# Output products of an attention kernel one unit later, with their operands a unit ahead and the weights' operands spread between the adds

## The reference

```
x  = hidden states, 4 batches x 512 tokens x 1024, f32
xn = layernorm(x)
qkv = xn @ w_qkv             32 query heads, 8 key and 8 value heads, 128 wide
scores = q k^T / sqrt(128) - slope(head) * sqrt(distance), causal
attn = softmax(scores) @ v
out = x + attn @ w_o + (xn @ W^T + b + the chosen low-rank term of xn)
```

## Time and profile before

| | |
|---|---|
| three runs | 2558.04, 2558.14 (median), 2559.82 us |
| the profiled execution | 2558.13 us, its span 2556.3 us |
| PE busy | 2429.0 us, 95% |
| DVE busy | 1593.5 us, 62% |
| ACT busy | 1442.5 us, 56% |
| POOL busy | 884.0 us, 35% |
| granted PE clock, mean | 0.987 |

### The profile page before, as it was taken

One profiled execution on the slowest core, in us unless ns is written; L12 is line 12 of the kernel. 1 busy time (PEld: TensorE's weight loads), 2 busy tenths in 40 slices (PEclk: granted clock), 3 DMA queues, 4 the chain that ended last, 5 costly groups with the idle time before them and its releaser, 6 DMA issues.

```text
span 2556.3 us, 35119 instructions
## 1 busy us (share of the span) xinstructions
PE 2429.0 (95%) x12128; PEld 2042.3 (80%) x12128; DVE 1593.5 (62%) x2905; ACT 1442.5 (56%) x3131; POOL 884.0 (35%) x1158
## 2 busy tenths in 40 slices
PE   6999999997999999998899999999999999999998
PEld 4787888885778888887788888888888888888886
DVE  6657445565756445654666777667766776667765
ACT  4432133334533133333877777777777777777774
POOL 3211000001231000000464556545654556445654
PEclk8999999998999999999999999999999999999999
DMA  4546354464355435445613231332334231332221
GB/s 148 183 132 222 116 191 159 176 219 176 103 159 202 153 137 198 169 176 189 227 67 116 102 121 68 115 116 100 110 146 182 100 116 67 124 115 101 80 108 69
DMA packets 94704, 355.25 MB, mean 139 GB/s; under 512 B 8874, under 2 KB 9018, under 8 KB 85569
## 3 DMA queue, kind: packets, MB, share of 16 engines
q1 hardware_dynamic: 62480, 233.43, 25.5%
q0 software_dynamic: 32048, 119.60, 13.5%
HBM read 235.02 MB, written 117.97 MB: 138 GB/s over the span
## 4 chain that ended last, share of the span: by engine, by line
PE 79%; DVE 10%; issue 5%; ACT 4%; DMA 1%; POOL 1%; ACTq 0%; DVEq 0%; SPq 0%; POOLq 0%
PE ps L648 25%; PE ps L650 25%; PE ps L649 25%; PE ps L835 4%; DVE wo L1130 3%; DVE acc L1398 1%; ACT probs L1049 1%; DVE probs L1367 1%; DVE pt_lo L1130 1%; ACT wo L895 1%; ACT res_hi L895 1%; DVE stats L1144 1%; ACT rows L924 1%; DVE w_lo L1130 1%; DMA qk_s<-res_hi 0%
## 5 line engine op out<-in xcount | busy, mean ns | idle before, releaser
L895 ACT ACTIVATE w_hi<-raw 128x1024 fp32r<-128x1024 f32 x196 | 207.0, 1059 | 559.3 <-PE ps L650 440.8
L1130 DVE TENSOR_TENSOR w_lo<-raw,w_hi 128x1024 fp32r<-128x1024 f32 x196 | 239.1, 1224 | 358.2 <-ACT w_hi L895 358.1
L1398 DVE TENSOR_TENSOR acc<-ps,acc 128x512 f32<-128x512 f32 x448 | 296.7, 684 | 226.7 <-issue 195.4
L648 PE MATMUL ps<-x_hi,w_hi 128*128 128x512 f32 x1120 | 436.3, 390 | 0.0
L650 PE MATMUL ps<-x_hi,w_lo 128*128 128x512 f32 x1120 | 435.8, 389 | 0.0
L649 PE MATMUL ps<-x_lo,w_hi 128*128 128x512 f32 x1120 | 435.7, 389 | 0.0
L648 PE MATMUL ps<-wo,op_hi 128*128 128x512 f32 x896 | 367.0, 410 | 50.4 <-issue 30.6
L1035 ACT ACTIVATE probs<-probs,neg_max 128x512 f32<-128x512 f32 (+3 forms) x512 | 283.6, 565 | 200.8 <-DVE neg_max L1367 200.8
L650 PE MATMUL ps<-wo,op_lo 128*128 128x512 f32 x896 | 354.8, 396 | 0.0
L649 PE MATMUL ps<-wo,op_hi 128*128 128x512 f32 x896 | 353.1, 394 | 0.0
L1367 DVE CUSTOM_DVE_ANT_0 probs<-ps,bias 128x512 f32<-128x512 f32 (+3 forms) x512 | 220.3, 484 | 95.3 <-PE ps L650 93.3
(11 more groups left out here) (156 smaller groups left out, 4983.9 us busy)
## 6 DMA issues: line engine op xcount, KB each, us to landing
raw<-w_all SPq DMA_DIRECT2D x70, 1024.0 KB, 5.5
q<-qk_s SPq DMA_DIRECT2D x128, 512.0 KB, 3.3
qk_s<-res_hi POOLq DMA_DIRECT2D x40, 1024.0 KB, 4.6
wo_raw<-w_o SPq DMA_DIRECT2D x64, 512.0 KB, 5.5
qk_s<-res_a POOLq DMA_DIRECT2D x20, 1024.0 KB, 9.1
qk_s<-res_b POOLq DMA_DIRECT2D x20, 1024.0 KB, 5.3
k<-qk_s SPq DMA_DIRECT2D x32, 512.0 KB, 5.7
v<-v_s SPq DMA_DIRECT2D x32, 512.0 KB, 8.5
```

The lines of the kernel that those rows point to most:

```text
L648: pe.matmul(to, st_hi, mv_hi, start=start, stop=False, skip_group_check=True)
L895: nc.scalar.activation(to, source, ACT.Copy).then_inc(signal, 1)
L1130: nc.vector.tensor_tensor(to, source, high.bitcast(F32), ALU.subtract).then_inc(signal, 1)
L1398: nc.vector.tensor_tensor(to, fill[f % 2][:, :], to, ALU.add).then_inc(s_acc, 1)
```

## The change

The order of the units stays (pair of batches, key head, batch, head; `unit` is written in another way), and so do the number and shape of all instructions. What moves:

- `fills`: each part is one unit later. The four parts of a set that were at places 1 and 5 are now at places 2 and 6, and so on; the loop has one more turn at its end.
- `shaped`: all `op_hi` and `op_lo` and the differences of a part are made in the unit ahead of it; nothing is made in its own unit.
- the weights: highs of steps 0, 1 at the end of place 4 (before: 3); 3, 2 at the end of 5; 4, 5 at the start of 6, ahead of the first exponential; 6 at the end of 6. Lows of 0, 1 and 3 at the end of place 5 (there are three parts there); step 2 at place 6 behind `pt_lo`; 4 between the adds of place 6; 5 and 6 behind its last add. Sums: 4 at place 3, 2 and 3 at place 4, 5 at place 5. Before: lows 0, 1 at the end of 3; 2, 3, 4 at the end of 4; 5, 6 at the end of 5.
- SP's issue of the next group's blocks keeps its place in the program (place 7), and its condition.
- the running sums go out and come in a tile pair at a time, in turns of SP of their own.

```
-OUT_SPLITS = ((), (0, 1), (2, 3, 4), (5, 6))
-WO_SUMS_IN = ((4,), (2,), (3, 5), ())
+WO_SUMS_IN = {7: (4,), 8: (2, 3), 9: (5,)}
+WO_ORDER = (0, 1, 3, 2, 4, 5, 6)
+HIGHS_FIRST = {10: (4, 5)}
+HIGHS_LAST = {8: (0, 1), 9: (3, 2), 10: (6,)}
+LOWS_EARLY = {10: (2,)}
+LOWS_MIDDLE = {9: (0, 1), 10: (4,)}
+LOWS_LAST = {9: (3,), 10: (5, 6)}
...
         def fills(n):
-            s, c = (n - 1) // G - 1, (n - 1) % G
+            s, c = (n - 2) // G - 1, (n - 2) % G
...
         def shaped(n):
-            s, c = n // G - 1, n % G
...
+            s, c = (n - 1) // G - 1, (n - 1) % G
...
+            return s, [OUT_SUMS[i] for i in SUM_SHARES[c]], list(SHARES[c])
...
+        def making(n, table):
+            group, place_ = (n - 3) // GROUP_UNITS, (n - 3) % GROUP_UNITS + 7
+            return [(group, i) for i in table.get(place_, ())] if 0 <= group < GROUPS else []
...
-                if n % (2 * G) == G + 3 and group + 1 < GROUPS:
+                if n % GROUP_UNITS == 7 and group + 1 < GROUPS:
...
             (ACT)
                 if 2 <= n < UNITS + 2:
                     outputs(n - 2)
-                for part in at_once:
-                    out_high(*part)
+                for part in making(n, HIGHS_FIRST):
+                    out_split(*part)
                 if 1 <= n < UNITS:
                     exponential(n, 0)
...
             (DVE)
                 if 1 <= n <= UNITS:
                     transposed(n - 1)
+                for part in making(n, LOWS_EARLY):
+                    out_split(*part)
                 if n < UNITS:
                     inverses(n)
-                for f in todo[1:]:
+                for f in todo[1:3]:
                     add_fill(*f)
-                for part in out_splits(n):
+                for part in making(n, LOWS_MIDDLE):
+                    out_split(*part)
+                for f in todo[3:]:
+                    add_fill(*f)
+                for part in making(n, LOWS_LAST):
                     out_split(*part)
```

More of the change, by code:

```diff
@@ L324, in op_source, with made @@
             return {0: b11, 1: b21, 5: b22}.get(k, op_raw[:, part])
[L328 to L343, removed]
+        def making(n, table):
+            group, place_ = (n - 3) // GROUP_UNITS, (n - 3) % GROUP_UNITS + 7
+            return [(group, i) for i in table.get(place_, ())] if 0 <= group < GROUPS else []
         def summed(group, step):
             return len(WO_SUMS) * group + WO_SUMS.index(step) + 1
+        def made(group, step):
+            return STEPS * group + WO_ORDER.index(step) + 1
         def used(group, step):
-            return PARTS * (2 * group - 1) + STEPS + step + 1
+            return PARTS * (SETS // GROUPS * group - 1) + STEPS + step + 1
         def wo_source(step):
@@ L438, in out_weights, with sums_home @@
                         out_block(group + 1, i)
[L440 to L456, removed]
+            def sums_home(pr, b, t):
+                return bass.ds((pr * TT + b * QT + t) * P, P)
@@ L477, in _ @@
                 out_weights(n)
[L478 to L482, removed]
+                sums_in_and_out(n)
+            for n in range(UNITS, UNITS + 3 * G):
+                sums_in_and_out(n)
             for tt in range(TT):
@@ L617, in wo_sums @@
                 last.then_inc(s_wo_sum, 1)
[L619 to L628, removed]
-                    pool.wait_ge(s_at_raw, G * (s + 1))
-                    for tile, k in OUT_SUMS[2:4]:
-                        out_sum(s, tile, k)
-                for part in at_once:
[L633 to L641, removed]
+            for n in range(UNITS + G + 2):
+                s, new_sums, new = shaped(n)
+                if new_sums:
+                    pool.wait_ge(s_at_raw, G * (s + 1))
+                for tile, k in new_sums:
+                    out_sum(s, tile, k)
+                for part in new:
+                    out_low(s, part)
+                for group, step in making(n, WO_SUMS_IN):
                     wo_sums(group, step)
@@ L1112, in _ @@
                         exponential(n, c)
-                for part in later:
-                    out_high(*part)
+                for part in new:
+                    out_high(s, part)
                 if n < UNITS:
                     normalise(n)
-                for part in out_splits(n):
+                for part in making(n, HIGHS_LAST):
                     out_split(*part)
@@ L1400, in out_split @@
             def out_split(group, step):
-                dve.wait_ge(s_wo_hi, STEPS * group + step + 1)
+                dve.wait_ge(s_wo_hi, made(group, step))
                 if step == 2:
```

74 lines of the change are left out of this document (43 added, 31 removed).

## The result

The changed kernel takes 2734.95 us (median of four runs, 2731.83 to 2738.01) against 2558.98 for the kernel before, a ratio of 1.068 (95% interval 1.067 to 1.070): 176 us slower. The forecast was 2700. The execution profiled after took 2737.3 us, its span is 2735.5, its mean granted clock 0.954.

The account below looks back on a forecast made before the run. PE, busy 2429.0 of 2556.3 us, was taken as the bound, so only its gaps could be won. To 2558 us came 103 for the groups, 36 for the clock and 3 for the edges: 2700 us, range 2612 to 2740.

Parts of the forecast that it names:

- Places 4 and 5: Units at these places run without waits for late operands or late maxima, at 10.43 and 9.03 us.
- the old 4.9 us: PE time lost per group at places 4, 5 and 6 of the kernel before, all to be removed.
- First wait: PE at place 6 waits 6.0 us for the low of step 2 before its third product; bounds 4.0 and 6.6.
- Place 7: Late maxima behind the last two lows of the weights cost 0.7 us here.
- Second wait: Scores at place 0 of the next group wait 5.1 us for q, queued behind the weight blocks; bounds 4.0 and 6.5.
- Clock: PE's clock falls once, 1.17 us, behind each of the two new waits: +36 us; bounds 0 and twice this.
- Sum: Per group 4.9 us removed and 11.8 added, net +6.9; for 15 groups +103 us.
- Edges: Head +3, tail -3 and change of pairs +3 us, together +3 us.
- Rival A: Both new waits come but the clock stays at 2.4 GHz: 2664 us; chance 0.20.
- B: Place 0's scores do not wait, since the loads come through in time: 2606 us; chance 0.08.
- D: Faster: step 5's sum is off the path, place 6 waits 3.5 us, q in time, clock kept: 2540 us; chance 0.06.
- C: No change to speak of: 4.0 us wait at place 6, no clock lost, q in time: 2558 us; chance 0.04.

Follow-up runs that it names:

- experiment 1: Changed kernel with SP's issue of the next group's weight blocks moved from place 7 to place 0, behind k, q and v: 2624.81 us.
- experiment 9: Changed kernel with the blocks issued at place 0 behind k, q and v, and the weights' sums, highs and lows reordered: 2506.76 us.
- experiments 3 and 4: Changed kernel with the weights' work in its old order, one place later; blocks issued at place 7 (2734.49 us) or place 0 (2614.68 us).
- experiment 5: Changed kernel with highs and lows of steps 0 and 1 moved to the middle of place 4: 2754.86 us.
- experiment 2: Changed kernel with ACT's high of step 5 moved from ahead of place 6's first exponential to the end of place 6: 2700.7 us.

## Why the prediction was right, and by how much it was off

- **Places 4 and 5** at 10.43 and 9.03, no wait for `op_lo`: as said. All of the old 4.9 us went.
- **First wait**, taken as 6.0 where the walk gave 6.3: 6.4 in every whole group. The links were the ones named (POOL's lows, sum 5, high 5, exponential, `pt_hi`, `pt_lo`, low 2), and the sum ended 7.0 us into place 6, the late end of the bound, not 6.7. The Trainium skill (SBUF — State Buffer, SBUF: two separate sides) has DVE, when it reads two inputs from SBUF, and POOL block each other for whole instructions. The rows agree, in that nothing overlapped: from 1535.67 to 1543.60, 7.93 us, DVE made three lows and POOL two lows and a sum, and alone these take 3 x 1.22 + 1.4 + 2.84 = 7.9. The rounding down to 6.0 "since the collided row shows some overlap" was the wrong choice, by 0.4. The row had also lost more than the 1.0 that I read from it: POOL's next sum, at 1488.46 in the kernel before, took 3.79 in place of 2.84 beside the same two lows.
- **Place 7**: 0.6 without the second wait (9.59 against 9.03 in experiment 1), 0.7 said.
- **Second wait**: 5.1 said; 5.5 on average (place 7 with it lasts 15.10, less 9.03 and 0.6), 5.82 in the group shown. The issue, said at 3.4 us, came at 3.25, but `q` took 9.8 us to land in place of 8.7. For the 0.15 us that I added for the semaphore I had no row; the scores start within 0.1 us of the landing.
- **Clock**: the term that was mis-sized. I took one fall of 1.17 us for each wait, from the earlier trace rows. Measured: place 6 lasts 18.8 on average, 10.43 + 6.4 + 2.0; place 0 lasts 12.76, 10.43 + 2.3. So 4.3 us a group in place of 2.3, near the upper bound (twice): some 65 us and not 36. (About 0.3 of the 2.0 is not the clock: place 6 of experiment 9 loses as much beside its wait at a clock of 1.00.) The row was taken behind a wait of 2 us; behind the two of 5 to 6 us the loss was nearly twice as much each.
- **Sum**: 77.8 + 6.4 + 0.6 + 5.5 + 4.3 = 94.6 us a group, as the 14 whole groups measure on average; I had 82.75 + 6.9 + 2.3 = 92.0. The 2.6 us between them, 2.0 of them the clock's, are 37 us for 14 whole groups, and the profiled execution is 37 above the forecast.
- **Edges**: the head lasts 49.4 us (1237.09 to 1286.47) in place of 43.3, +6 where I said +3; the last group, from its start to the end of the span, lasts 124.3 in place of 116.7, 4.2 less than a whole group's 11.8 more, where I said 3.
- **Rival A** (the clock stays) is refuted by the 0.82 and 0.78; **B** and **D** by the two gaps; **C** by all of these. What rival B would have been worth is now known: experiment 1 took the second wait away and gained 110 us, not the 94 of 15 x 6.3, mostly because of the clock.
- What the prediction did not see: the first wait comes from how the operands, made a unit ahead, and the weights' sums, highs and lows stand in one another's queues, and not from this spreading of the lows alone. The old order fails too (experiments 3 and 4), and experiment 9, with the operands as far ahead, is 53 us faster than the kernel before; my own first guess, that the old order one place later would be near 2550, was wrong by 65 us.

## What to carry to other kernels

When work is moved in a hand-ordered schedule, walk each queue that it is moved past by due times: ahead of an instruction that the bound engine needs soon, nothing may stand that is needed later, however idle that engine is on average (POOL was 33% busy here, and ACT's high waited 3.00 us for its sum). A load that waits for a condition belongs behind the loads that don't, or the condition's delay is handed to all of them. And price a stall of the matrix engine with the clock that it loses, taken from a stall of about the same length. And when an instruction is moved to relieve one queue, look at what it now stands ahead of on the others (experiment 5).

## What the runs showed of the hardware

- What PE loses behind a gap, beyond the gap, is not in proportion to it. Behind 1.2 us (experiment 9) the matmuls go on at 0.23 us apart at a granted clock of 1.00; behind 2.0 us 1.2 or nothing; behind 4.0 (experiment 2, place 6 at 17.0) 2.6; behind 6.4 it is 2.0, and behind 5.5, at place 0, 2.3. It also varies for one gap: 1.5 to 3.0 from group to group behind the 6.4.
- A wait of SP's queue for the last low of a group, and `w_o` in front of `k` and `q`: 3.25 us into place 7 became 15.6 us until the scores could start, with the DMA at 264 GB/s over the place.
- Instructions of DVE that read PSUM ran beside POOL at their usual time (the first maxima 0.68 us at 1540.67 during POOL's sum, as alone); the 448 adds of the changed kernel, which have one input in PSUM, took 0.69 us at most. Those with two inputs in SBUF did not keep theirs (1.22 to 1.76 us for one low of 128x1024).
